# Mamba scan and mixture of experts on one core: seven drives made token by token on ScalarE and turned by TensorE, their decays kept in SBUF

## What is computed

```python
x_conv = silu(conv(x @ W_in[:, :256]))            # u, 256 channels
dt = softplus(x_conv @ W_dt + b_dt)
def step(h, ins):
    u_t, dt_t, B_t, C_t = ins
    dA = jnp.exp(dt_t[:, :, None] * A)            # the decay
    h = dA * h + (dt_t * u_t)[:, :, None] * B_t[:, None, :]   # the drive
    y_t = jnp.einsum('bdn,bn->bd', h, C_t)
    return (h, y_t)
...
y = (y + x_conv * D) * silu(z)
return y @ W_out
```

## Time and profile before

| | |
|---|---|
| median of 3 runs (lowest, highest) | 399.19 us (398.62, 399.43) |
| profiled execution: time, span | 398.69 us, 397.0 us |
| units 0 to 63 on VectorE | about 24.8 to 269.6 us of the span |
| busy over the span: TensorE, VectorE, ScalarE, GpSimd | 72%, 75%, 48%, 67% |
| granted TensorE clock, mean | 0.853 of 2.4 GHz |

### The profile page before, as it was taken

How to read it: one execution, slowest core, us unless ns; L and a number is a source line. 1 busy time by engine, 2 the same in 40 slices (tenths; PEclk the granted TensorE clock), 3 DMA queues, 4 the chain that set the end, 5 groups by cost and what they waited for, 6 DMA issues and landing times. The chain is left out here.

```text
span 397.0 us, 4746 instructions
## 1 busy us (share of the span) xinstructions
PE 287.0 (72%) x1420; PEld 200.6 (51%) x1420; DVE 297.2 (75%) x443; ACT 190.4 (48%) x372; POOL 266.2 (67%) x226
## 2 busy tenths in 40 slices
PE   8976798487686838775745799577088999998800
PEld 6435455364573524564433453224087888887600
DVE  2698799989999999979999999996403333334466
ACT  2846576575745595573554254571302222232405
POOL 5416488976878799897879894888440455556732
PEclk9998699969889877969555699999679999999955
DMA  7061079463234444221212231001134444221873
GB/s 229 5 213 53 1 233 265 139 199 110 82 112 120 147 146 142 81 68 53 100 60 75 79 113 54 1 7 35 34 95 131 118 113 117 81 87 53 243 217 113
DMA packets 35784, 42.87 MB, mean 108 GB/s; under 512 B 3862, under 2 KB 26331, under 8 KB 35760
## 3 DMA queue, kind: packets, MB, share of 16 engines
q1 hardware_dynamic: 32336, 37.38, 31.3%
q0 software_dynamic: 2304, 4.24, 3.2%
q10 hardware_dynamic: 1120, 0.97, 0.8%
HBM read 30.11 MB, written 12.79 MB: 108 GB/s over the span
## 5 line engine op out<-in xcount | busy, mean ns | idle before, releaser
L1277 POOL TENSOR_TENSOR product<-state,c_wide 128x1024 f32<-128x1024 f32 x64 | 149.7, 2344 | 51.9 <-DVE state L1505 31.8
L955 ACT ACTIVATE psum<-dt,a_neg 128x512 f32<-128x512 f32 x124 | 85.2, 689 | 100.2 <-DVE state L1505 97.2
L606 PE MATMUL psum<-ident,product 128*128 128x128 f32 x384 | 65.9, 330 | 37.0 <-POOL product L1277 36.9
L606 PEld LDWEIGHTS psum<-ident,product 128*128 128x128 f32 x384 | 55.3, 171 | 55.4 <-POOL product L1277 51.2
L1505 DVE TENSOR_TENSOR_SCAN state<-psum,carry,drive 128x512 f32<-128x512 f32 x64 | 79.7, 1269 | 2.0 <-ACT psum L955 1.8
L1484 DVE TENSOR_TENSOR drive<-dtu,psum 128x1024 f32<-128x1024 f32 x64 | 76.6, 1197 | 5.2 <-PE psum L592 5.1
L1505 DVE TENSOR_TENSOR_SCAN state<-psum,drive 128x512 f32<-128x512 f32 x64 | 75.5, 1208 | 3.2 <-ACT psum L955 2.7
L1398 POOL DMA_INDIRECT result_rows<-state,result_at x30 | 30.3, 1011 | 40.3 <-DVE state L1719 33.0
L1352 POOL DMA_INDIRECT slot_rows<-sent,scatter_at x32 | 32.6, 1018 | 10.9 <-issue 10.9
L808 PE MATMUL psum<-product,fc_sb 128*128 128x320 f32 x128 | 36.1, 435 | 1.1 <-DVE product L1687 1.1
L1684 DVE TENSOR_SCALAR tags<-c_wide 128x10 f32<-128x10 f32 x8 | 1.3, 164 | 43.0 <-PE psum L797 43.0
(11 more groups left out here) (241 smaller groups left out, 451.7 us busy)
## 6 DMA issues: line engine op xcount, KB each, us to landing
c_wide<-c_rows SPq DMA_DIRECT2D x32, 512.0 KB, 4.0
slot_rows<-blank SPq DMA_DIRECT2D x8, 325.0 KB, 4.7
c_wide<-slot_rows SPq DMA_DIRECT2D x8, 325.0 KB, 3.5
result_rows<-zeros SPq DMA_DIRECT2D x8, 256.0 KB, 5.1
late_rows<-zeros SPq DMA_DIRECT2D x8, 256.0 KB
fc_sb<-in_c_fc SPq DMA_DIRECT2D x8, 256.0 KB
proj_sb<-in_c_proj SPq DMA_DIRECT2D x8, 256.0 KB
c_wide<-result_rows SPq DMA_DIRECT2D x8, 256.0 KB
```

Of the source, the lines that this page charges most:

```text
L606: last = nc.tensor.matmul(y_part(j, d), product[:, i, d, j * P:(j + 1) * P], ident[:, :], is_transpose=True, start=False, stop=True, skip_ ...
L955: nc.scalar.activation(psum[:, A_BANK + d, :], dt[:, q % 2, d, :], ACT.Exp, scale=a_neg[:, n:n + 1]).then_inc(decay_ready, 1)
L1277: nc.gpsimd.tensor_tensor(product[:, U % PRODUCTS, channels, :], state[:, U % RING, channels, :], wide, ALU.mult).then_inc(product_ready, 1)
```

## The change

Seven units (`TURNED`: 4, 7, 10, 14 in the first chunk, 53, 57, 60 in the last) get their drive without VectorE. With tokens on the partitions, B's value is one number for each partition. So ScalarE scales `dtu_t`, a copy of dtu turned to token order, by it (`drive_by_token`, four instructions of 256 elements, three units ahead), and TensorE turns each half back into a bank of the two for B (`turn_drive`, four transposes for each half). The scan reads it from PSUM. The decays of these units go to an SBUF buffer in one instruction, two units ahead (three for unit 4, four for unit 14), so that the following unit's can be made two units ahead in PSUM. B and dtu are turned once for each of the two chunks (`turn_b`, `turn_first_dtu`, `dtu_job`) and copied by ScalarE (`take_b`, `take_first_dtu`, `take_dtu`). `silu_u(2)` moves from unit 15 to unit 12, and in the third chunk the taking of dt's second half and `soften_exp` stand one unit sooner.

```diff
+TURNED = (4, 7, 10, 14, 53, 57, 60)
+AHEAD = {4: 3, 14: 4}
...
+            def turn_drive(U, d):
+                pe.wait_ge(drive_t_ready, TPC * (TURNED.index(U) + 1))
+                pe.wait_ge(drive_ready, drive_number(U) + d)
+                for j in range(TPC):
+                    last = nc.tensor.transpose(psum[:, turned_bank(U, d), j * P:(j + 1) * P], drive_t[:, j, d * P:(d + 1) * P], ident[:, :])
+                last.then_inc(drive_turned, 1)
...
+            pe.wait_ge(bc_rows_ready, 1)
+            turn_b(b_t_psum(Z_BANK, 0))
             turn_x(3)
...
-                if 2 <= U + 1 <= LAST:
-                    spread_b(U + 1)
+                if U in TURNED:
+                    turn_drive(U, 1)
+                elif U >= 1 and U - 2 not in TURNED and drive_beside(U):
+                    spread_b(drive_beside(U))
...
+                if U - 1 in TURNED:
+                    spread_b(drive_beside(U + 1))
+                if U + 1 in TURNED:
+                    turn_drive(U + 1, 0)
...
+                    if U in TURNED:
+
+                        if TURNED.index(U):
+                            act.wait_ge(scanned, DT * (TURNED[TURNED.index(U) - 1] + 1))
+                        nc.scalar.activation(decay_sb[:, :, :], dt[:, q % 2, :, :], ACT.Exp, scale=a_neg[:, n:n + 1]).then_inc(turned_decay_ready, DT)
+                        break
...
+                for j in range(TPC):
+                    nc.scalar.activation(drive_t[:, j, :], dtu_t[:, j, :], ACT.Copy, scale=b_t[:, j, n:n + 1]).then_inc(drive_t_ready, 1)
...
+                for T in TURNED:
+                    if T - AHEAD.get(T, 2) == U:
+                        decays(T)
+                    if T - 3 == U:
+                        drive_by_token(T)
...
-                    elif n == (5 if q == 2 else first + 2):
+                    elif n == first + 2:
                         take_dt_job(q + 1, 1)
-                    elif n == (6 if q == 2 else first + 3):
+                    elif n == first + 3:
                         soften_exp(q + 1)
...
                         take_z(2, n - 12)
+                        if n == 12:
+                            act.preload_act_table(ACT.Silu)
+                            silu_u(2)
+                            act.preload_act_table_set("natural_log_exp_and_others")
...
-                if U < LAST:
-                    drives(U + 1)
+                if drive_beside(U):
+                    drives(drive_beside(U))
```

More of the change, by code:

```diff
@@ L52, with drive_number, drive_beside @@
 FAR = tuple(U + 2 for U in PAUSES)
+TURNED = (4, 7, 10, 14, 53, 57, 60)
+AHEAD = {4: 3, 14: 4}
+def drive_number(U):
+    return U - sum(m < U for m in TURNED)
+def drive_beside(U):
+    if U in TURNED or U == LAST:
+        return None
+    return U + 2 if U + 1 in TURNED else U + 1
 def near(U):
-    return U - sum(m < U for m in FAR)
+    return U - sum(m < U for m in FAR + TURNED)
 class Tally:
@@ L635, in dt_job, with dtu_job @@
                 project_dt(q, r, bank).then_inc(made, 1)
+            def dtu_job(q, half):
+                bank, made = job_bank(f"t{q}{'ab'[half]}")
+                pe.wait_ge(dtu_ready, DT * (q + 1))
+                for j in range(2):
+                    for d in range(DT):
+                        t = (2 * half + j) * P
+                        last = nc.tensor.transpose(psum[:, bank, j * D_INNER + d * P:j * D_INNER + (d + 1) * P], dtu[:, q % 2, d, t:t + P], ident[:, :])
+                last.then_inc(made, 1)
             def conv_job(q, d, taps):
@@ L688, in project_out @@
                     last = nc.tensor.matmul(out_tile(q, j), x_chan[:, b, t:t + P], center[:, :], start=False, stop=True)
+                if q == 1 and pair == 0:
+                    pe.wait_ge(bc_rows_ready, NQ)
+                    turn_b(b_t_psum(bank, B_AT))
                 last.then_inc(made, 1)
@@ L933, in _, with take_b @@
                     nc.scalar.activation(bc_sb[:, :], psum[:, B_BANK + 1, :], ACT.Copy).then_inc(bc_rows_ready, 1)
+            def take_b(rows):
+                act.wait_ge(b_turned, 1 if rows is first_b else 2)
+                if rows is not first_b:
+                    act.wait_ge(drive_t_ready, TPC * sum(T < D_STATE for T in TURNED))
+                nc.scalar.activation(b_t[:, :, :].rearrange("p j n -> p (j n)"), rows, ACT.Copy).then_inc(b_t_ready, 1)
+            first_b = b_t_psum(B_BANK, 0)
+            take_b(first_b)
             copy_x(3)
@@ L984, in take_dt_job @@
                         act.wait_ge(decay_ready, DT * near(D_STATE * (q - 1)))
[L985 removed]
+                        act.wait_ge(far_decay_ready, DT * sum(U < D_STATE * (q - 1) for U in FAR))
+                        act.wait_ge(turned_decay_ready, DT * sum(U < D_STATE * (q - 1) for U in TURNED))
                 take_dt(q, d, rows).then_inc(taken, 1)
@@ L1031, in take_out @@
                 rows, taken = job_made(f"out{q}{'ab'[pair]}")
+                if q == 1 and pair == 0:
+                    take_b(rows[:, B_AT:B_AT + TPC * D_STATE])
                 tiles = slice(TPC * q + 2 * pair, TPC * q + 2 * pair + 2)
@@ L1504, in scan @@
                     before = carry[:, n, d:d + 1]
-                nc.vector.tensor_tensor_scan(state[:, U % RING, d, :], decay, drive[:, U % 2, d, :], before,
+                nc.vector.tensor_tensor_scan(state[:, U % RING, d, :], decay, rows, before,
                                              ALU.mult, ALU.add).then_inc(scanned, 1)
```

104 lines of the change are left out of this document (85 added, 19 removed).

## The result

| | before | changed |
|---|---|---|
| median (lowest, highest) | 398.90 us of 4 runs (397.58, 399.43) | 391.51 us of 4 runs (390.25, 393.26) |
| ratio, 95% interval | | 0.9837 (0.9805 to 0.9869) |
| profiled execution: time, span | 398.69, 397.0 us | 392.27, 390.5 us |
| units end on VectorE at | 269.60 us | 263.07 us |

The kernel is faster by 1.6%. The spans differ by 6.5 us and the ends of the units by 6.53, so all of the gain lies in the 64 units, and what follows them only moved. The forecast was 8.7 us. The medians are 7.4 us apart, since the profiled execution of the changed kernel is 0.8 us above its median.

What follows compares the result with a forecast made beforehand. VectorE's own work plus its few waits was taken to bound the 64 units; 4.7 + 0.8 + 3.2 = 8.7 us off 398.69 gave 390.0 us profiled, 390.5 as median, range 386.9 to 395.0.

Steps and rivals of the forecast that it cites:

- Turned drives of 1.11 us: Seven drives taken off VectorE at 1.11 us each, 7.8 us: 4.4 in the first chunk, 3.3 in the last.
- removed waits of 5.2 us: VectorE's waits at units 4, 6 and 17, 2.47 + 0.90 + 1.84, would go: 5.2 us at most.
- The rival by which the drives were not it: GpSimd or TensorE would fill each gap and only the silu waits go, 2 to 4 us: 396; chance 0.03.
- 4.7 us net up to unit 17: First chunk and unit 17: 9.6 us possible gain less 4.9 us of new waits, 4.7 us net.
- The new waits: VectorE in units 3, 5, 6, 7, 9, 12, 13, 15 would wait 0.4 to 0.9 us each, 4.9 in sum.
- The start: Before unit 0: no cost if TensorE stays fast; convolution at 19.3 us, spreading at 23.4, just ahead of the drive at 23.52.
- the bound of 0.06: Turned units' scans on VectorE: 1.12 us each, uncertain by 0.06 a step, at most 0.8 us over 14 scans.
- four scaled copies: ScalarE's four scaled copies for a turned unit take 1.7 us, bounds 1.1 and 2.0.
- the term 0.8 of the sum: Third chunk: the sooner copy of dt gains 0.8 us, between 0 and 1.9, as unit 41 gives most back.
- the last chunk: Last chunk: three drives, 3.3 us, less 0.1 lost on TensorE, gain 3.2 us.
- The clock rival: TensorE's clock, low at the B and C job and perhaps the first convolution, takes back half: 394.5 us; chance 0.20.

Runs made afterwards that it cites:

- e1_first: Changed kernel with only the first chunk's units 4, 7, 10, 14 turned, the last chunk's three drives on VectorE again; 395.84 us, 0.9921 of the kernel before.
- e3_dt_late: Changed kernel with dt's second half and its exp taken one unit later again in the third chunk; 391.95 us, 0.9845 of the kernel before.
- e7_sends_late: Changed kernel with GpSimd's two sends of units 35 and 36 moved three units later, to units 38 and 39; 386.55 us, 0.9748 of the kernel before.
- e10_before_sends: Kernel before with GpSimd's two sends of units 35 and 36 three units later, nothing of the change; 397.01 us, 0.9998 of the kernel before.
- e11_dt_sends: Changed kernel with the two sends of units 35 and 36 late and the third chunk's dt taken one unit later; 390.89 us, 0.9849 of the kernel before.
- e4_spread41: Changed kernel with unit 41's spreading issued one place sooner, in unit 39 ahead of the projection; 389.96 us, 0.9796 of the kernel before.
- e5_spread3: Changed kernel with the spreadings for units 24, 41 and 54 issued one place sooner; 386.88 us, 0.9734 of the kernel before.
- e9_sends_spread2: e7_sends_late with the spreadings for units 24 and 54 issued one place sooner; 386.22 us, 0.9732 of the kernel before.
- e2_last: Changed kernel with only the last chunk's units 53, 57, 60 turned, the first chunk's drives on VectorE again; 400.53 us, 1.0048 of the kernel before.
- e12_last_again: The kernel of e2_last run again on another chip; 397.62 us, 1.0002 of the kernel before.

## Why the prediction was right, and where it was off

- **Right: what bounds the units.** VectorE's own work and its waits. Turned drives of 1.11 us and removed waits of 5.2 us came out; in the first and the last chunk nothing else became the bound. The rival by which the drives were not it gave 396; the last chunk's three drives alone made 3.3 (e1_first).
- **Right: the first chunk.** Forecast 4.7 us net up to unit 17, measured 4.9. The new waits stand where the walk put them: in order, with the forecast in brackets, unit 3 0.74 (0.9), unit 5 0.59 (0.6), unit 6's drive 0.45 (0.4, at 43.84 where 43.5 was forecast), unit 7's second scan 0.95 (0.9), units 9, 12, 13 and 15 0.42, 0.30, 0.27 and 0.49 (0.5 to 0.6 each). The start cost 0.1: the convolution at 19.54 with 3.60 us, unit 0's drive at 23.64. That is less than the start differs between runs: unit 0's first scan lies between 24.22 and 24.98 us in the fourteen traces.
- **Right: the unknown durations.** Turned scans are 2.30 us for two, where two others take 2.33, so a step is 1.11 and within the bound of 0.06; four scaled copies 1.69 (1.7).
- **Not priced: the second chunk.** It lost 0.5 us, of which no term spoke. No run lays that on the change: with TensorE's clock at 1.00 there, as e7_sends_late has it, the same instructions gain 0.8 us on the trace of before, and so does e10_before_sends, which has the kernel before's own instructions there.
- **Off: the third chunk,** the term 0.8 of the sum, in the step "I take 0.8, nearer the low end since TensorE still idles there before the product". It lost 0.7, below the lower end of 0, and unit 41's drive came at 175.34 where 173.0 was named. That unit 41 gives back what unit 39 gains was right and is shown by e3_dt_late. What the step missed is that unit 41 gives back more. From the start of adding product 37 to the spreading took 4.13 us before and 4.89 after. 0.35 of it is `turn_b` for the last chunk, which the change puts ahead of this very spreading and which I had counted only at the start; 0.4 is the projection, now wholly at half clock (2.77 against 2.37 us). So 1.93 us were gained at unit 39, 2.81 lost at unit 41 and 0.63 at unit 35, and a wait of 0.37 for a carry near 202 us is gone: -1.1, of which 0.4 come back in steps that I didn't follow. And I had not asked what sets product 37: "GpSimd has no gap there" was read as a fact of its load, and was in truth two sends, 2.4 us, that could move.
- **Nearly right: the last chunk,** 2.85 us for 3.2: unit 54's spreading stands behind four matmuls of L625 that take 3.56 us, and VectorE waits 0.95; before, the same four took 3.29 us and it waited 0.69.
- **The sum:** 4.9 - 0.5 - 0.7 + 2.85 = 6.55 us, against 4.7 + 0.8 + 3.2. The time of 391.51 is 1.0 above the forecast of 390.5, which flatters it: in the profiled executions 2.2 of the 8.7 us are missing, and the units end at 263.07 where 260.9 was named. The median lies nearer by what single executions differ, and that is luck.
- **The clock rival** did not come where it was placed: the clock was 1.00 in the first chunk, the job for B and C took 1.98 us, not 3.8. The transposes of the turned drives ran four in 0.60 us, as fast as those of the earlier trace rows. The Trainium skill (TensorE: Matmul & The Clock Gate, Part 4, PE-mode transpose) has the full clock not engage for transposes; between the matmuls of this stretch the trace does not bear that out. Whether transposes keep the full clock without matmuls among them no run shows: from 196 to 213 us, where they are most of the work, the clock is 0.60 with TensorE busy 9.7 of 17.0 us. At half clock TensorE was in the third chunk, behind idle time.

## What to carry to other kernels

When work is taken off the engine that sets the time, list for the next chunks the latest arrival at each of its waits, down to the engine that has no gap (here GpSimd's sends): the gain ends there, and an instruction that was free before the change has a price after it. A wait that can be moved by one place (a spreading issued sooner, a copy taken sooner) gains only if its own last arrival moves; with the sends late the same copy of dt was worth 1.9 us in the traces. A small addition for a later chunk must be charged at the place in the queue where it is issued.

## What was not expected of the hardware

**TensorE's clock differs between runs where the instructions are the same.** Up to unit 35 the changed kernel and e7_sends_late have the same program. The stretch 84 to 108 us, of the changed kernel and then of e7_sends_late:

```profile
84.00:96.00 12.00, 9.84 (x45) 6.32 (x46) 11.85 (x11) 7.03 (x13) 9.61 (x7) 0.86 0.50 154
96.00:108.00 12.00, 8.61 (x52) 7.35 (x51) 11.28 (x10) 7.94 (x13) 9.00 (x4) 0.78 0.35 135
```

```profile
84.00:96.00 12.00, 9.42 (x55) 6.39 (x55) 12.00 (x11) 7.14 (x12) 9.61 (x7) 1.00 0.44 136
96.00:108.00 12.00, 8.33 (x65) 6.87 (x64) 12.00 (x11) 7.52 (x12) 8.60 (x4) 1.00 0.45 137
```

At 0.86 and 0.78 VectorE waits 0.18 and 0.70 us; at 1.00 it doesn't, and from unit 17's first scan to unit 32's it takes 58.56 and 57.25 us. So up to 1.3 us between single profiles can be this, and not an edit. From 84 to 96 us eight traces have the same instructions: the changed kernel, e1_first, e3_dt_late and e11_dt_sends have 0.86, and e4_spread41, e5_spread3, e7_sends_late and e9_sends_spread2 have 1.00. What decides it was not tested.

**A late DMA can cost twice.** In e2_last and e12_last_again 2.2 to 2.3 us of idle TensorE were followed by 16 matmuls at half clock, 2.5 to 2.9 us more. The twelve other traces have 0.33 us or less of the same wait (e1_first 0.26), and 4.54 or 4.55 us for the 16 matmuls.
